# Channel means of the edge filter as f32 products in 32-column groups, and tables of two layers loaded one stage earlier

## The chip, the cores and the metric

The kernel runs on one core of a Trainium2 chip. The metric is the device time of one execution in microseconds (us), lower is better. Three timed executions of the kernel before are shown, and one more was taken with the profiler.

## The reference, cut to what matters

The input x is 16 images of 32 channels of 64x64 in f32. Four layers are applied in turn, each as `x = x + conv(groupnorm(x))` with 16 groups of two channels. The convolutions are a spectral mixing (L0), the edge filter (L1), a 5x5 filter (L2) and a full-size circular filter (L3). The change is in L1. From the normalised x (here `x`) it takes

```python
x_mean = x.mean(axis=1, keepdims=True)                 # over the 32 channels
gx = conv(x_mean, sobel_x); gy = conv(x_mean, sobel_y) # 3x3, zero padding
edge = jnp.sqrt(gx * gx + gy * gy + 1e-06)
edge_strength = edge.reshape(B, 1, ht, P, wt, P).mean(axis=(3, 5))   # P = 8
edge_strength = edge_strength - edge_strength.min(axis=(2, 3), keepdims=True)
edge_norm = edge_strength / (edge_strength.max(axis=(2, 3), keepdims=True) + 1e-06)
edge_coeff = 1.0 + EDGE_BOOST * edge_norm
...
xf = jnp.fft.rfft2(x_patch)          # 8x8 patches
xf = xf * mask * scaling             # scaling from edge_coeff, per patch
out = jnp.fft.irfft2(xf, s=(P, P))
```

So the edge map of an image needs the mean over its channels at every pixel before the first patch can be filtered.

## The kernel before, in words

All of x stays in the on-chip tile `X`, 128 partitions (4 images by 32 channels) by Q = 4 groups by 4096 pixels. Each layer's normalisation is two numbers per partition and group, `rstd` (scale) and `shift`, so that the normalised value is `X * rstd + shift`. The program is a row of stages. Each stage is a block with one hand-written queue for each engine, and no engine enters the next block before all have left this one. In order: kernel spectra (with the statistics of the input), statistics `n0`, L0 forward, L0 mix, L0 inverse (`i0`), statistics `n1`, edge stage, L1 filter stage, statistics `n2`, L2, statistics `n3`, L3 forward, L3 mix, L3 inverse. Since the order inside a stage is written out by hand, nothing moves unless the code moves it.

`stats_stage` makes `rstd` and `shift` by one small product on PE and seven small steps on DVE and ACT. On SP it can also load tables (`loads`) and copy tiles (`copies`), and SP then waits for all of them. `n1` gets seven tables of the edge filter and four copies of the L2 weights, `n3` gets six tables of L3.

The edge stage (`l1_edge_stage`) goes through 32 chunks of 512 pixels, group by group. For each chunk ACT normalises into `e1_src` (L278), DVE rounds it to f16 into `hi` (L1229, shown as `e_high_part`), and DVE (even chunks) or POOL (odd ones) takes the rest `lo16` (L1195, `e_low_part`). PE multiplies each part by a 128-column window of the table `wide` in f16 that puts the means of this group's four images and of this strip of eight rows on the right 4 of 128 partitions (L1165); two narrow products of 64 columns fetch the rows above and below for the strips next to it (L1169, L1172). All sums are in PSUM banks 0 and 1. Ahead of them stand 16 transposes that only keep PE busy (`keep_warm`, L210). When all four groups are done, DVE copies the sums into `m` (L1234, L1235), with a frame of zeros, and the Sobel filter, the root, minimum and maximum follow in a row of small dependent steps that ends with the copy into `edge` (L1269).

`l0_forward_stage` collects its results in two halves by turns (`xm[q % 2]`): one is a tile of its own, the other lies in `y`.

In names of the trace `e_`, `ks_`, `f_`, `l_`, `i_`, `m_`, `c_` are prefixes of tiles by stage, `bank` is PSUM.

## Time and profile before

| | us |
|---|---|
| three timed executions | 951.16, 938.11, 948.60 |
| their median | 948.6 |
| the profiled execution, whole | 947.15 |
| its span, first to last instruction | 945.3 |
| outside the span (947.15 - 945.3) | 1.85 |
| mean granted TensorE clock | 0.923 of full |

The profiled execution lies 1.45 us below the median. The three timed ones lie 13 us apart. The stages in question stand in the span at 316.5 to 324.6 us (`n1`), 324.6 to 378.3 us (edge stage) and 641.1 to 645.8 us (`n3`).

### The profile page before, as it was taken

How to read it: one execution, taken by the hardware profiler on the slowest of the kernel's cores; microseconds unless marked ns; L12 is line 12 of the kernel's file. 1: busy time of each engine (PE TensorE's matmuls, PEld its weight loads, DVE VectorE, ACT ScalarE, POOL GpSimd, SP SyncE). 2: the span in 40 equal slices, each digit the busy share in tenths (PEclk: the TensorE clock that was granted, in tenths of full speed). 3: DMA queues.
4: the chain of work that ended last, by engine and by line, in shares of the span. 5: the costliest groups of instructions: out<-in, count | busy, mean ns of one | idle time of the engine just before them, and what ended most of it. 6: DMA issues, size and time to landing. Idle time of an engine off the chain costs nothing. (4 is left out here: it accounts for less than half of the span.)

```text
span 945.3 us, 28083 instructions
## 1 busy us (share of the span) xinstructions
PE 775.2 (82%) x11423; PEld 647.9 (69%) x11423; DVE 620.4 (66%) x1144; ACT 480.7 (51%) x800; POOL 108.9 (12%) x96
## 2 busy tenths in 40 slices
PE   7999996874699464887599999966888489889997
PEld 7999995764588342766444444435777488889997
DVE  3455445778476697689687776775666677756453
ACT  0133336864434270754579997005887557764200
POOL 0000000110100162456003223000000100000000
PEclk9999998997699797899799999997999888999985
DMA  8599968750000100000000000004000448840054
GB/s 314 199 316 383 314 200 213 184 117 4 2 0 0 41 1 0 2 0 0 1 1 1 1 1 1 1 1 107 1 0 0 89 91 176 180 89 1 1 206 155
DMA packets 48380, 80.25 MB, mean 85 GB/s; under 512 B 19874, under 2 KB 38312, under 8 KB 43448
## 3 DMA queue, kind: packets, MB, share of 16 engines
q1 hardware_dynamic: 31672, 62.49, 23.8%
q10 hardware_dynamic: 16640, 16.78, 5.2%
q8 instruction: 52, 0.85, 0.4%
q14 instruction: 16, 0.13, 0.0%
HBM read 50.74 MB, written 27.92 MB: 83 GB/s over the span
## 5 line engine op out<-in xcount | busy, mean ns | idle before, releaser
L1618 DVE SCALAR_TENSOR_TENSOR X<-bank,c_power,X 32x512 f32 x128 | 96.7, 756 | 36.5 <-PE bank L1568 32.9
L1761 PE MATMUL bank<-m_xp,m_kf 128*32 128x64 f32 x2048 | 81.4, 245 | 22.2 <-DVE m_xp L1696 11.1
L1761 PEld LDWEIGHTS bank<-m_xp,m_kf 128*32 128x32 f32 x2048 | 80.3, 171 | 23.4 <-issue 23.3
L415 DVE COPY ks_rows<-bank 128x512 f32<-128x512 f32 x64 | 41.3, 687 | 67.3 <-PE bank L345 67.3
L215 DVE BATCH_NORM_STATS2 bn<-X 128x6 f32 x128 | 83.0, 683 | 2.9 <-POOL X L1358 1.6
L433 ACT COPY ks_spec<-bank 128x512 f32<-128x512 f32 x64 | 34.3, 589 | 98.8 <-PE bank L360 96.1
L1524 ACT ACTIVATE c_r<-X,c_nrm 32x1024 f32 (+1 forms) x56 | 75.0, 1340 | 2.4 <-DVE c_nrm L1592 1.1
L345 PE MATMUL bank<-ks_fw,ks_src 64*128 64x64 f32 x1024 | 68.7, 298 | 6.3 <-DMA ks_src<-in_L_conv_weights 6.3
L360 PE MATMUL bank<-ks_fh,ks_rows 64*128 64x128 f32 (+1 forms) x1152 | 72.5, 281 | 0.2 <-ACT ks_spec L433 0.2
L345 PEld LDWEIGHTS bank<-ks_fw,ks_src 64*128 64x128 f32 x1024 | 68.1, 215 | 6.2 <-issue 6.2
L360 PEld LDWEIGHTS bank<-ks_fh,ks_rows 64*128 64x128 f32 (+1 forms) x1152 | 67.6, 184 | 3.3 <-issue 1.8
L620 DVE TENSOR_TENSOR f_tl<-bank,f_th 128x512 f16<-128x512 f32 x64 | 42.3, 682 | 19.3 <-ACT f_th L571 19.3
L1782 ACT COPY xm<-bank 64x512 f32 (+1 forms) x64 | 33.0, 595 | 39.1 <-PE bank L1761 39.1
L1568 PE MATMUL bank<-c_rh,c_w_high_odd 128*64 128x512 f16 (+1 forms) x288 | 48.0, 385 | 3.8 <-DVE c_rl L1510 3.8
L1568 PE MATMUL bank<-c_rh,c_w_high 128*64 128x512 f16 (+1 forms) x288 | 48.4, 387 | 1.6 <-DVE c_rl L1510 1.6
L488 PE MATMUL bank<-c_l_fw,f_th 128*128 128x64 f16 (+1 forms) x256 | 37.5, 207 | 13.1 <-DVE f_tl L620 13.1
L1568 PE MATMUL bank<-c_rh,c_w_low 128*64 128x512 f16 (+1 forms) x288 | 47.7, 382 | 0.0
L1568 PE MATMUL bank<-c_rl,c_w_high 128*64 128x512 f16 (+1 forms) x288 | 47.6, 382 | 0.0
L1309 PE MATMUL bank<-mm,p_tt 64*128 64x128 f32 x512 | 38.7, 293 | 10.8 <-DVE X L1341 6.7
L1568 PE MATMUL bank<-c_rl,c_w_high_odd 128*64 128x512 f16 (+1 forms) x288 | 47.6, 382 | 0.0
L1568 PE MATMUL bank<-c_rh,c_w_low_odd 128*64 128x512 f16 (+1 forms) x288 | 47.5, 382 | 0.0
L630 DVE TENSOR_TENSOR f_cl<-bank,f_ch 128x512 f16<-128x512 f32 x48 | 32.3, 688 | 22.5 <-ACT f_ch L585 22.4
(201 smaller groups left out, 1838.9 us busy)
## 6 DMA issues: line engine op xcount, KB each, us to landing
ks_src<-in_L_conv_weights SPq DMA_DIRECT2D x16, 1024.0 KB, 6.9
kf<-ks_spec ACTq DMA_DIRECT2D x16, 1024.0 KB, 8.9
m_kf<-kf SPq DMA_DIRECT2D x32, 512.0 KB, 8.4
X<-in_x SPq DMA_DIRECT2D x4, 2048.0 KB, 12.6
out_y<-X SPq DMA_DIRECT2D x32, 256.0 KB, 2.5
l_wb<-in_L_conv_weights_r SPq DMA_DIRECT2D x4, 512.0 KB, 11.1
l_wb<-in_L_conv_weights_i SPq DMA_DIRECT2D x4, 512.0 KB, 13.7
xf<-f_xm SPq DMA_DIRECT2D x16, 112.0 KB, 3.2
```

The costliest lines, as they stand in the source:

```text
L215: dve.bn_stats(self.bn[:, c, :], self.X[:, q, c * CH:(c + 1) * CH]).then_inc(step, 1)
L345: last = pe.matmul(ps[2 * g + r][:, c * N:(c + 1) * N], src[p][at, C // 4 * g + c, m], fw[at], start=True, stop=True)
L360: return pe.matmul(banks[j][0:slots * C, to:to + P], rows[p][half, m, at:at + slots].rearrange("p s c -> p (s c)"), mats[half, part], star ...
L415: dve.tensor_copy(rows[p][:, m, :, C // 2 * g + r:C // 2 * (g + 1):2], ps[2 * g + r][:].rearrange("p (c n) -> p n c", n=N)).then_inc(rows_ ...
L433: c = act.copy(spec[p][:, 2 * u:2 * u + 2, :, j:IB:2].rearrange("p f t m k -> p f m t k"), ps[4 + 2 * (u % 2) + j][:].rearrange("p (f m t ...
L488: pe.matmul(to, h, m[:, 0], start=True, stop=False)
L620: dve.tensor_tensor(self.tl[j % 4][:], ps[j % 4][:], self.th[j % 4][:], ALU.subtract).then_inc(self.turned_read, 1)
L1309: m = pe.matmul(ps[2 + 2 * (j % 2) + h][:, k * P:(k + 1) * P], tt[j % 2][at, k * P:(k + 1) * P], mm[at, :, at], start=True, stop=True)
L1524: act.activation(to, of, ACT.Identity, scale=nrm[at, 0, bass.ds(q, 1)], bias=nrm[at, 1, bass.ds(q, 1)]).then_inc(ready[b], 1)
L1568: return pe.matmul(ps[2 * n + (oy + odd) % 2][2 * oy * C:2 * (oy + 1) * C, :], w[rows, ky, kx, 2 * oy:2 * oy + 2].rearrange("p o c -> p (o ...
L1618: dve.scalar_tensor_tensor(x, of.rearrange("p (y x) -> p y x", x=HN), filt.power[at, 2:3], x, ALU.mult, ALU.add).then_inc(added, 1)
L1761: last = pe.matmul(ps[4 * half + m // 8][at:at + C, m % 8 * N:(m % 8 + 1) * N], kf[p][:, j, :, H * half + m], xp[half][:, j, m].rearrange( ...
```

## The change

It has three parts.

1. The means are made from `X` itself, in f32. The weights are the table `wide` times `rstd` of the group (four DVE steps, before any product), so scale and mean are one product; the part of `shift` is one number per image, made by four one-column products with a new table `l1_shift`, and added by DVE when the sums leave PSUM (`sh`, with a new table `l1_rows` that leaves it out beyond the border). The weights are 32 columns wide instead of 128: strip s writes only the 32 partitions of its pair of strips, in the order s = 0, 2, 4, 6, 1, 3, 5, 7, so that one product after another goes to another group of 32 columns. ACT's normalising, DVE's rounding and the low parts on DVE and POOL are gone.
2. The tables and copies of `n1` are issued by SP at the start of the stage before (`inverse_stage`), and the six tables of `n3` at the end of SP's queue in the first stage.
3. To make room for L3's tables, `xm` of `l0_forward_stage` lies wholly in `y`, and ACT's wait for the stores of the kernel spectra stands ahead of q = 0 instead of q = 1.

```diff
@@ l0_forward_stage
-        xm = [pr.sb(ctx, "f0_xm", [P, 2, S, KX, 2, IB]),
-              y.rearrange("p t x r b -> p (t x r b)")[:, 0:size].rearrange(
-                  "p (t s x r b) -> p t s x r b", t=2, s=S, x=KX, r=2)]
+        xm = [y.rearrange("p t x r b -> p (t x r b)")[:, g * size:(g + 1) * size].rearrange(
+            "p (t s x r b) -> p t s x r b", t=2, s=S, x=KX, r=2) for g in range(2)]
...
-                    if s == 0 and q == 1:
+                    if s == 0 and q == 0:
@@ inverse_stage, SP
+                for t, n in loads:
+                    sp.dma_start(t[:], pr.ins[n]).then_inc(next_const, 16)
+                for to, of in copies:
+                    sp.dma_start(to, of).then_inc(next_const, 16)
+                sp.wait_ge(next_const, 16 * (len(loads) + len(copies)))
@@ l1_edge_stage, ACT
-                with act.Fori(0, Q) as q:
-                    for j in range(NCH):
-                        act.wait_ge(split[j % 2], START + HC * (q - 1) + j // 2 + 1)
-                        pr.normalise(act, src, q, j, ready)
@@ l1_edge_stage, PE
                 pr.keep_warm(pe, 16)
-                pe.wait_ge(zeroed, 3)
...
-                            w = wq[p][:, 124 - B * s:124 - B * s + P]
-
-                            pe.wait_ge(split[s % 2], START + HC * q + s // 2 + 1)
-                            for part in (hi, lo16):
...
+                order = [2 * g + k for k in range(2) for g in range(PS // 2)]
+
+                def mean(q, s, to, of):
+
+                    at = slice(s // 2 * 2 * B, (s // 2 + 1) * 2 * B)
+                    first = 124 - s % 2 * B
+                    return pe.matmul(to[at, :], wq[:, q, first:first + 2 * B], of, start=q == 0 and s in started,
+                                     stop=False, skip_group_check=True)
+
+                for q in range(Q):
+                    pe.wait_ge(window, q + 1)
+                    rows = pr.X[:, q, :].rearrange("p (h w) -> p h w", w=N)
+                    started = (0, 2, 4, 6)
+                    for s in order:
+                        mean(q, s, ps[0], pr.X[:, q, s * CH:(s + 1) * CH])
+                    started = (1, 2, 4, 6)
+                    for s in order:
+                        if s > 0:
+                            mean(q, s, ps[1][:, 0:N], rows[:, ROWS * s - 1, :])
+                    started = (0, 2, 4, 6)
+                    for s in order:
+                        if s < PS - 1:
+                            last = mean(q, s, ps[6][:, 0:N], rows[:, ROWS * s + ROWS, :])
+                for q in range(Q):
+                    last = pe.matmul(ps[3][:, 0:1], shift_m[:, q * P:(q + 1) * P], pr.shift[:, q:q + 1],
+                                     start=q == 0, stop=q == Q - 1)
+                last.then_inc(meant, 1)
@@ l1_edge_stage, DVE
+                for q in range(Q):
+                    dve.tensor_scalar(wq[:, q], wide[:, 12 - IB * q:12 - IB * q + 252], pr.rstd[:, q:q + 1], None,
+                                      ALU.mult).then_inc(window, 1)
...
-                        for j in range(NCH):
-                            at = slice(j * CH, (j + 1) * CH)
-                            dve.wait_ge(ready, NCH * q + j + 1)
-                            dve.tensor_copy(hi[:, q, at], src[:, at]).then_inc(high, 1)
-                            if j % 2:
-                                low_part(dve, q, j - 1)
-                dve.wait_ge(meant, START + Q)
+                dve.wait_ge(meant, 1)
+                dve.tensor_scalar(sh[:], shift_rows[:], ps[3][:, 0:1], None, ALU.mult).then_inc(zeroed, 1)
                 dve.wait_ge(zeroed, 3)
-                dve.tensor_copy(m[:, 1:1 + ROWS, 1:1 + N], ps[0][:].rearrange("p (h w) -> p h w", w=N))
...
+                dve.tensor_scalar(m[:, 1:1 + ROWS, 1:1 + N], ps[0][:].rearrange("p (h w) -> p h w", w=N),
+                                  sh[:, 0:1], None, ALU.add)
+                dve.tensor_scalar(m[:, 0, 1:1 + N], ps[1][:, 0:N], sh[:, 1:2], None, ALU.add)
+                then(dve.tensor_scalar(m[:, HALO - 1, 1:1 + N], ps[6][:, 0:N], sh[:, 2:3], None, ALU.add))
@@ four_layers
-                kernel_spectra_stage(pr, fwd_loads + inv_loads, filt)
+                kernel_spectra_stage(pr, fwd_loads + inv_loads + last_loads, filt)
...
-                pr.stats_stage("n1", mean_loads + table_loads, filt.odd_copies())
+                pr.stats_stage("n1")
...
-                pr.stats_stage("n3", fwd_loads + inv_loads)
+                pr.stats_stage("n3")
```

On DVE the edge stage begins like this in the kernel before (L1204 is the stage's start; the tiles `e_` are its own). Of the two groups written out in the loop the first rows stand here:

```order
L1214 MEMSET e_m 128x660
L1215 MEMSET e_eps 128x1
L1216 MEMSET e_nought 128x256
L1220 UNCONDITIONAL_BRANCH
L1220 ISA
L1225 REGISTER_ALU
L1225 ISA
L1225 COPY e_wq<-c_l_mean 128x252
L1228 ISA
L1229 ISA
L1229 COPY e_high_part<-e_src 128x512
```

and like this in the changed kernel, up to the first step of the Sobel filter:

```order
L1196 TENSOR_SCALAR e_wq<-c_l_mean,rstd 128x252 x4
L1198 MEMSET e_m 128x660
L1199 MEMSET e_eps 128x1
L1201 TENSOR_SCALAR e_sh<-c_l_rows,bank 128x3
L1203 TENSOR_SCALAR e_m<-bank,e_sh 128x8x64
L1205 TENSOR_SCALAR e_m<-bank,e_sh 128x64
L1206 TENSOR_SCALAR e_m<-bank,e_sh 128x64
L1208 SCALAR_TENSOR_TENSOR e_v<-e_m 128x640
```

The weights of all four groups come first now, no chunk step is left, and three additions of `sh` stand where two copies stood.

PE's queue in the edge stage of the kernel before, from the transposes to the second chunk's first part:

```order
L210 MATMUL bank<-ident 128x128 x16
L1152 MATMUL bank<-e_nought 128x512
L1153 MATMUL bank<-e_nought 128x128
L1155 UNCONDITIONAL_BRANCH
L1155 ISA
L1162 ISA
L1165 ISA
L1165 MATMUL bank<-e_high_part,e_wq 128x512
L1165 REGISTER_ALU
L1165 MATMUL bank<-e_low_part,e_wq 128x512
L1165 ISA
L1165 MATMUL bank<-e_high_part,e_wq 128x512
```

and in the changed kernel, from the transposes to the product with the gains:

```order
L215 MATMUL bank<-ident 128x128 x16
L1147 MATMUL bank<-X,e_wq 32x512 x8
L1147 MATMUL bank<-X,e_wq 32x64 x14
L1147 MATMUL bank<-X,e_wq 32x512 x8
L1147 MATMUL bank<-X,e_wq 32x64 x14
L1147 MATMUL bank<-X,e_wq 32x512 x8
L1147 MATMUL bank<-X,e_wq 32x64 x14
L1147 MATMUL bank<-X,e_wq 32x512 x8
L1147 MATMUL bank<-X,e_wq 32x64 x14
L1165 MATMUL bank<-shift,c_l_shift 128x1 x4
L1170 MATMUL bank<-e_gain,c_l_band 128x1
```

There are 32 wide products instead of 64 and 56 narrow ones instead of 112, with 32 output partitions each, in one run without a wait for another engine's chunk.

SP's queue in the changed kernel from the start of `i0` (L837) to the gains of the edge stage:

```order
L837 UNCONDITIONAL_BRANCH
L840 DMA c_l_mean<-in_l_mean 128x264
L840 DMA c_l_pick<-in_l_pick 128x128
L840 DMA c_l_spread<-in_l_spread 16x512
L840 DMA c_l_shift<-in_l_shift 128x512
L840 DMA c_l_rows<-in_l_rows 128x3
L840 DMA c_l_dft<-in_l_dft 128x128
L840 DMA c_l_same<-in_l_same 128x128
L840 DMA c_l_band<-in_l_band 6x128
L840 DMA c_l_high<-in_l_high 128x1
L842 DMA c_w_high_odd<-c_w_high 64x1152
L842 DMA c_w_low_odd<-c_w_low 64x1152
```

These stood between the branches of `n1` before, without `c_l_shift` and `c_l_rows`.

## Rows read from the trace of the kernel before

**Rows 1.** Busy time of the engines while the means are made

```profile
core 0: us, PE busy (x) PEld busy (x) DVE busy (x) ACT busy (x) POOL busy (x), PEclk, DMA share, GB/s
324.57:363.50 38.93, 26.46 (x195) 17.82 (x195) 36.68 (x55) 24.40 (x32) 22.76 (x16) 0.94 0.00 1
```

**Rows 2.** Groups of instructions by form between 324 and 364 us

```profile
L1229 DVE CAST e_high_part<-e_src 128x512 f32 x32 | 23.6, 775 | 0.0
L1195 DVE TENSOR_TENSOR e_low_part<-e_src,e_high_part 128x512 f32 x16 | 10.9, 678 | 0.0
L1225 DVE CAST e_wq<-c_l_mean 128x252 f16 x4 | 4.0, 990 | 0.2 <-issue 0.2
```

**Rows 3.** Timeline in order of time, n1 into the edge stage

```profile
318.56 0.16 DVE L270 SCALAR_TENSOR_TENSOR shift<-gm,rstd 128x4 f32<-128x4 f32 x1
...
321.53 0.60 SPq L243 DMA_DIRECT2D c_w_low_odd<-c_w_low  x1
...
324.61 3.65 PE L210 MATMUL bank<-ident 128*128 128x128 f32 x16 [7.43 <-PEq L237]
```

**Rows 4.** Timeline, n2 into L2, where n2 loads nothing

```profile
455.89 0.16 DVE L270 SCALAR_TENSOR_TENSOR shift<-gm,rstd 128x4 f32<-128x4 f32 x1
...
456.35 5.77 PE L210 MATMUL bank<-ident 128*128 128x128 f32 x26 [1.84 <-PEq L237]
```

**Rows 5.** Timeline, n3 into L3 forward

```profile
643.14 0.16 DVE L270 SCALAR_TENSOR_TENSOR shift<-gm,rstd 128x4 f32<-128x4 f32 x1
643.43 0.43 SPq L241 DMA_DIRECT2D c_l_iw<-in_l_iw  x1
...
645.83 1.91 DVE L609 TENSOR_SCALAR f_src<-X,rstd,shift 128x512 f32<-128x512 f32 x4 [2.53 <-PEq L237]
```

**Rows 6.** Timeline, the end of the means

```profile
363.37 0.19 PE L1172 MATMUL bank<-e_low_part,e_wq 128*128 x1
...
363.60 0.69 DVE L1234 COPY e_m<-bank 128x512 f32<-128x512 f32 x1 [1.91 <-PE bank L1172]
...
364.52 0.83 DVE L1238 SCALAR_TENSOR_TENSOR e_v<-e_m 128x640 f32<-128x640 f32 x1
```

**Rows 7.** PE's timeline, f32 products: weights of 128 columns, then two halves of the rows

```profile
304.04 7.07 PE L916 MATMUL bank<-c_l_iw,i_tt 128*128 128x256 f32 x32
...
384.34 1.16 PE L1309 MATMUL bank<-mm,p_tt 64*128 64x128 f32 x16
```

**Rows 8.** PE's timeline, L3 mix: f32 products with 32-column weights

```profile
805.78 9.70 PE L1761 MATMUL bank<-m_xp,m_kf 128*32 128x64 f32 x256 [1.79 <-DMA m_kf<-kf]
```

**Rows 9.** Busy time in stretches of L1761 (762 to 775) and L1054 (898, 918)

```profile
762.50:775.00 12.50, 12.50 (x334) 12.40 (x332) 10.55 (x24) 10.43 (x16) 0.00 (x0) 1.00 0.47 97
...
898.00:902.00 4.00, 4.00 (x153) 4.00 (x149) 0.70 (x2) 0.00 (x0) 0.00 (x0) 1.00 0.02 4
918.00:922.00 4.00, 4.00 (x82) 4.00 (x84) 2.48 (x4) 0.00 (x0) 0.00 (x0) 0.50 0.50 184
```

**Rows 10.** Busy time of L1568's instructions alone (f16, 512 columns, two 64-column groups)

```profile
500.00:510.00 10.00, 10.00 (x110) 4.90 (x108) 1.00 0.01 2
```

**Rows 11.** Busy time at the start of the edge stage, after it, in i0

```profile
325.00:328.90 3.90, 3.90 (x19) 3.40 (x18) 3.67 (x9) 3.90 (x6) 1.39 (x1) 0.51 0.01 2
328.92:363.00 34.08, 21.65 (x171) 13.65 (x170) 32.77 (x47) 20.39 (x27) 21.37 (x15) 1.00 0.00 1
...
250.00:316.00 66.00, 58.40 (x382) 53.39 (x380) 41.64 (x76) 26.26 (x48) 4.29 (x12) 0.97 0.00 0
```

**Rows 12.** Timelines of SP, PE and ACT, first stage to L0 forward

```profile
120.71 0.43 SPq L330 DMA_DIRECT2D c_l_iw<-in_l_iw  x1
...
145.84 0.36 PE L249 MATMUL bank<-st,pair 128*128 128x8 f32 x2 [2.75 <-PEq L307]
...
152.24 0.34 SPq L670 DMA_DIRECT2D l_wb<-in_L_conv_weights_r  x1
...
166.22 0.36 ACT L715 COPY f_xm<-bank 128x224 f32<-128x224 f32 x1
```

More of the change, by code:

```diff
@@ L132, in constants @@
     out["l1_mean"] = wide
+    image = np.arange(P) // C
+    out["l1_shift"] = np.concatenate([np.tile(np.eye(B)[IB * q + image] / C, (1, PS)) for q in range(Q)], 1)
+    strip = np.arange(P) // B
+    out["l1_rows"] = np.stack([np.ones(P), strip > 0, strip < PS - 1], 1)
     out["l1_pick"] = np.stack([np.eye(P)[:, 16 * s:16 * s + 16] for s in range(PS)], 1).reshape(P, P)
@@ L802, in _, with inverse_stage @@
                 pool.memset(y[:, :, KX:].rearrange("p s x r b -> p s (x r b)"), 0.0)
-def inverse_stage(pr, name, y, slots, modes, mats, rows4, last):
+def inverse_stage(pr, name, y, slots, modes, mats, rows4, loads, copies):
     nc, ps = pr.nc, pr.psum
@@ L823, in inverse_stage @@
                                               ("made", "made_read", "turned2", "turned2_read"))
-    pixels, added, step, stored = (pr.sem(f"{name}_{n}") for n in ("pixels", "added", "step", "stored"))
+    pixels, added, step, next_const = (pr.sem(f"{name}_{n}") for n in ("pixels", "added", "step", "next_const"))
     padded = pr.sem(f"{name}_padded")
-    out_groups = pr.out.rearrange("(q b) c h w -> q (b c) (h w)", b=IB)
     with ExitStack() as ctx:
@@ L835, in _ @@
             def _(sp):
-                if last:
-                    with sp.Fori(0, Q) as q:
-                        for part in range(4):
-                            sp.wait_ge(added, START + NCH * q + NCH // 4 * (part + 1))
-                            at = slice(part * PIX // 4, (part + 1) * PIX // 4)
-                            sp.dma_start(out_groups[q][:, at], pr.X[:, q, at]).then_inc(stored, 16)
-                    sp.wait_ge(stored, 16 * 4 * Q)
+                for t, n in loads:
[3 more added lines that the diff above has]
+                sp.wait_ge(next_const, 16 * (len(loads) + len(copies)))
             def stage(eng, q, s):
@@ L930, in _ @@
                         dve.tensor_tensor(x, x, ps[4 + c % 4][:], ALU.add).then_inc(added, 1)
-                        if not last and c:
+                        if c:
                             dve.wait_ge(added, START + NCH * q + c)
                             pr.chunk_stats(dve, q, c - 1, step)
-                    if not last:
-                        dve.wait_ge(added, START + NCH * q + NCH)
-                        pr.chunk_stats(dve, q, NCH - 1, step)
-                        pr.group_stats(dve, q, step)
+                    dve.wait_ge(added, START + NCH * q + NCH)
+                    pr.chunk_stats(dve, q, NCH - 1, step)
+                    pr.group_stats(dve, q, step)
             @block.scalar
@@ L1109, in l1_edge_stage @@
     nc, ps = pr.nc, pr.psum
-    ready, window, meant = (pr.sem(f"e1_{n}") for n in ("ready", "window", "meant"))
+    window, meant = (pr.sem(f"e1_{n}") for n in ("window", "meant"))
     seq, root, picked, spread = (pr.sem(f"e1_{n}") for n in ("seq", "root", "picked", "spread"))
-    zeroed, high = pr.sem("e1_zeroed"), pr.sem("e1_high")
-    split = [pr.sem(f"e1_split{p}") for p in range(2)]
-    HC = NCH // 2
+    zeroed = pr.sem("e1_zeroed")
     gained, mask, mats = (pr.sem(f"e1_{n}") for n in ("gained", "mask", "mats"))
@@ L1117, in l1_edge_stage @@
     with ExitStack() as ctx:
-        src = pr.sb(ctx, "e1_src", [P, PIX])
-        hi, lo16 = (pr.sb(ctx, f"e1_{n}", [P, Q, PIX], F16) for n in ("high_part", "low_part"))
-        wide, pick, spread_m = means
+        wide, pick, spread_m, shift_m, shift_rows = means
         dft, same, band, high_mask = tables
         gain, mk, md = pr.sb(ctx, "e1_gain", [NB, 1]), pr.sb(ctx, "e1_mk", [P, 2]), pr.sb(ctx, "e1_md", [P, 2, P])
-        wq = [pr.sb(ctx, f"e1_wq{p}", [P, 252], F16) for p in range(2)]
+        wq = pr.sb(ctx, "e1_wq", [P, Q, 252])
+        sh = pr.sb(ctx, "e1_sh", [P, 3])
         m = pr.sb(ctx, "e1_m", [P, HALO, N + 2])
@@ L1131, in l1_edge_stage @@
         sq_eps = pr.sb(ctx, "e1_eps", [P, 1])
-        nought = pr.sb(ctx, "e1_nought", [P, CH], F16)
         with nc.Block() as block:
@@ L1190, in _ @@
                 last.then_inc(spread, 1)
-            def low_part(eng, q, j):
-                at = slice(j * CH, (j + 1) * CH)
-                eng.wait_ge(high, NCH * q + j + 1)
-                eng.tensor_tensor(lo16[:, q, at], src[:, at], hi[:, q, at], ALU.subtract).then_inc(split[j % 2], 1)
-            @block.gpsimd
-            def _(pool):
-                pool.sem_inc(split[1], START)
-                with pool.Fori(0, Q) as q:
-                    for j in range(1, NCH, 2):
-                        low_part(pool, q, j)
             @block.vector
```

52 lines of the change are left out of this document (12 added, 40 removed).

## The prediction

> **What bounds the kernel now.** The stages follow one another, with a barrier between them, so I read the two places that change on their own. First the busy time of the engines while the means are made [rows 1]: of 38.93 us DVE works 36.68, PE 26.46, ACT 24.40, POOL 22.76. The groups by form say on what [rows 2]: 32 roundings for 23.6 us, 16 low parts for 10.9, four tables for 4.0, together 38.5, the whole stretch. So DVE ends the means, and PE is fed by it. Then the timelines of the statistics stages. In `n1` the last arithmetic step, `shift`, starts at 318.56, but SP is still issuing at 321.53 and PE comes into the edge stage at 324.61 [rows 3]. In `n2`, the same stage with nothing to load, the step at 455.89 is followed by PE at 456.35 [rows 4]. In `n3` it stands at 643.14 and DVE starts at 645.83 [rows 5]. These waits for tables are bare time of the whole chip.
>
> **Part 1, tables out of n1 and n3.** From `shift` to the next stage n2 takes 0.46 us and n1 6.05 [rows 3, 4]: 5.6 us go. n3 takes 2.69 [rows 5]: 2.2 us go. What they cost elsewhere: SP does nothing in `i0`, and the DMA engines are idle there for 66 us (share 0.00) [rows 11]; nine loads and four copies at about 0.5 us of issue each need 7 us. In the first stage six more tables stand behind SP's last issue at 120.71 us and need some 3 us, while the next stage starts at 145.84; SP's next work is at 152.24 [rows 12]. Both cost 0. If the first stage's DMAs were late by the whole 3 us, it would still be covered by the 20 us that are left.
>
> **Part 2, `xm` in `y`.** ACT now waits for the kernel spectra's stores before its first `xm` copy, which stands at 166.22; SP, which waits for the same stores, has gone on at 152.24 [rows 12]. 14 us of cover, cost 0.
>
> **Part 3, the means.** ACT's, DVE's and POOL's chunk work goes away, and PE's own products become the path. PE starts at 319.0 (324.61 less 5.6), the 16 transposes take 3.65 us [rows 3], and the four DVE steps for the weights are done by then (even at the 0.99 us of the old ones [rows 2]; probably less). So products start at 322.7. Each group has 8 wide products (512 columns) and 14 narrow ones (64), all f32.
>
> An f32 product shows as two records: L916 has 16 products and 32 records of 256 columns in 7.07 us, 0.221 us each [rows 7]. For 512 columns that is 0.442 a record, 0.884 a product, if nothing overlaps. How much do the 32-column groups overlap? The nearest rows:
> - L1761 has the same form (128 rows, 32 columns of weights, f32), two groups by turns, 64 columns: 256 records in 9.70 us, 0.038 each [rows 8]. Without overlap 64 columns would be 0.055. Overlap 1.46.
> - L1309, two halves of the rows by turns, 128 columns: 16 records in 1.16 us, 0.073 each with the tail, against 0.110 [rows 7]. At least 1.5, nearer 2 in the steady part.
> - L1054, four row groups by turns, 64 columns: 153 records in 4.00 us, 0.026 each [rows 9]. Overlap 2.1, although four groups are there.
> - L1568, f16, 512 columns, two 64-column groups: 110 records in 10.00 us [rows 10], 0.091 each. One f16 pass of 512 columns is half of an f32 record, 0.221: overlap 2.4 (some records have fewer rows or are missing), so two full streams over 128 rows do run side by side.
>
> I take 2: wide streams like L1568's hide what is fixed in each record, and nothing with f32 goes above 2.1, with four groups by turns either. An order that would give such a cap: the two records of one product go to the same group, one after the other, and if starts keep the program's order, only the second record of one product meets the first of the next. A wide product is then 0.442 us and a narrow one 0.076 (two of L1761's records). Per group 8 x 0.442 + 14 x 0.076 = 4.60 us, four groups 18.4 us.
>
> Here the Trainium skill has a rule, "TensorE: Matmul & The Clock Gate", Part 3 (packing small matmuls): products in different 32-column tiles run at once, three of them 2.38 times as fast, and matmuls start and end strictly in order. By the 2.38 a wide product would take 0.37 us and the four groups some 16 us, an estimate from that page; no row here shows more than 2.1 with f32. The order it states is the one just described. That all tiles run at once is the rival "four at once" below.
>
> To add: the clock. Before, the granted clock was 0.51 (the 1.2 GHz level) until 328.9, 4.3 us after PE's start, and 1.00 after that [rows 11]. With the same 4.3 us PE would be at half speed to 323.3, 0.6 us into the products; since the moment varies I add 1.0 us. The four one-column products and the way out of PE: 0.5 us, an estimate from the 0.36 us that the one narrow product of a statistics stage takes [rows 12]. Sum 18.4 + 1.0 + 0.5: PE is done at 342.6. Before, its last product starts at 363.37, and the first Sobel step follows at 364.52 [rows 6], 1.15 us later; of this 0.69 is the wide copy and the rest the small one and latencies. Afterwards there is one step more ahead (`sh`, some 0.2 us) and one narrow step more: 1.3 us. The Sobel step starts at 343.9 instead of 364.5, so 20.6 us go, the 5.6 of n1 among them. What is late next is the chain of small steps that ends in `edge`; it is unchanged.
>
> With n3: 20.6 + 2.2 = 22.8 us. From the span 945.3 that leaves 922.5, and with 1.85 outside it **924.3 us**. The profiled execution lies 1.45 below the median of the timed ones, so on that scale it would be 925.8; I keep 924.3, since three runs 13 us apart don't carry that difference. From no change a measurement of this kernel can tell about 2%, 19 us.
>
> **Rivals.**
> - *Four at once.* All four column groups stream together: 0.221 a wide product, narrow ones 0.038. 8 x 0.221 + 14 x 0.038 = 2.3 a group, 9.2 in all, 9.2 less: 915.1. For it: the order of the strips lets it happen. Against: L1054's 2.1 with four groups.
> - *Little overlap.* The overlap of the only row in the same form, 1.46, holds for wide ones too: 0.605 each, 5.9 a group, 23.6 in all, 5.2 more: 929.5. For it: same form; two f32 streams over all 128 rows are in no other row. With none at all it is 8 x 0.884 + 14 x 0.110 = 8.6 a group, 34.4, 16 more: 940.3, and only DVE's ceiling has been exchanged for PE's. Against: L1761 itself is above 1.
> - *Slower than before: half clock and no overlap.* L1054, with a quarter of the rows at work, fell from clock 1.00 to 0.50 in the middle of its run and from 153 to 82 records in 4 us [rows 9]. If the 32-column products do that to PE while also serialised, a group costs 17.2 us and the means 68.8, 49.4 more than in my sum with its 1.0 for the clock: 973.7. It decides from 63 us for the means on (19.9 in my sum, 43 more); up to there the time is within 2% of before. Against: L1761, also with 32 columns, ran 12.5 us at 1.00 [rows 9]. Half clock with overlap would be 36.8, 17.4 more: 941.7, no slower than before.
> - *The loads don't leave the path*, because a table is late in its new place: 7.8 us less gained, 932.1. The idle DMA engines of `i0` speak against it.
>
> **How the numbers follow.** Forecast (overlap near 2) 0.60; four at once 0.12; overlap about 1.46 0.13; none, or half clock with overlap 0.09; loads stay on the path 0.03; half clock and no overlap 0.03 (slower). Beside these the end of the kernel is not steady: L1054 loses its clock at some moment, and in the whole of that stage a record costs 0.026 or 0.049 us, so with 1024 records it can move the time by some 10 us either way, about what the three runs show. So the forecast's own range is 917 to 932; with four at once below and little overlap above, the range for 8 in 10 is 913 to 936. Faster by over 2% means under 929.6. The forecast gives that with 0.85, four at once always, overlap 1.46 half the time: 0.51 + 0.12 + 0.07, that is 0.70. Slower by over 2%: 0.03. The rest, 0.27, is within 2%.
>
> **What the profile of the changed kernel would show.** From `shift` to PE's transposes 0.5 us in n1 and n3, as in n2. ACT and POOL idle during the means, DVE with four short steps. 64 wide and 112 narrow records of f32 on PE, the wide ones 0.22 us apart (0.11: four at once; 0.30: little; 0.44: none), and from the first to the last product some 19 us. DVE's wait for PE ahead of `sh` is the longest of the stage. A first Sobel step 25 us after PE's first transpose, against 40 before. The granted clock back at 1.00 within 5 us of PE's start. What would make me wrong: records further apart than 0.3 us, a clock of 0.5 through the products, or SP still busy when `i0` ends.

## The result, and the profile after

| | before | after |
|---|---|---|
| timed executions | 938.1 to 951.2, median 948.2 (4) | 905.4 to 914.1, median 909.8 (4) |
| ratio of the times | | 0.9618, 95% interval 0.9547 to 0.9689 |
| profiled execution, its span | 947.15, 945.3 | 905.9, 904.1 |
| mean granted clock | 0.923 | 0.938 |

The changed kernel is 38 us faster in this set. I had forecast 924.3 with a range of 913 to 936. Ratios and their intervals, here and below, leave out executions that lie more than 1.5% above the fastest of their kernel; the medians and spreads in the tables take in all.

The timeline of the kernel after, from the end of `n1` to the first Sobel step (start, duration, engine, line, operation; in brackets the idle time before it and its releaser):

```profile
316.46 0.16 DVE L275 SCALAR_TENSOR_TENSOR shift<-gm,rstd 128x4 f32<-128x4 f32 x1
...
316.93 3.65 PE L215 MATMUL bank<-ident 128*128 128x128 f32 x16 [1.84 <-PEq L242]
316.93 1.13 DVE L1196 TENSOR_SCALAR e_wq<-c_l_mean,rstd 128x252 f32<-128x252 f32 x4 [0.31 <-PEq L242]
...
320.50 8.86 PE L1147 MATMUL bank<-X,e_wq 128*32 128x512 f32 x176
...
322.25 0.57 PEld L1147 LDWEIGHTS bank<-X,e_wq 128*32 128x32 f32 x32 [0.30 <-issue]
323.01 0.23 PEld L1147 LDWEIGHTS bank<-X,e_wq 128*32 128x32 f32 x4 [0.20 <-issue]
323.44 0.23 PEld L1147 LDWEIGHTS bank<-X,e_wq 128*32 128x32 f32 x4 [0.20 <-issue]
323.87 0.23 PEld L1147 LDWEIGHTS bank<-X,e_wq 128*32 128x32 f32 x4 [0.20 <-issue]
...
329.29 1.05 PE L1165 MATMUL bank<-shift,c_l_shift 128*128 128x1 f32 x8
...
330.38 0.23 DVE L1201 TENSOR_SCALAR e_sh<-c_l_rows,bank 128x3 f32<-128x3 f32 x1 [11.61 <-PE bank L1165]
330.64 0.75 DVE L1203 TENSOR_SCALAR e_m<-bank,e_sh 128x512 f32<-128x512 f32 x1
...
331.81 0.83 DVE L1208 SCALAR_TENSOR_TENSOR e_v<-e_m 128x640 f32<-128x640 f32 x1
```

Set beside the rows of before:

- From `shift` to PE's first transpose: 0.47 us, as in `n2` (0.46 [rows 4]); before it was 6.05 [rows 3]. 5.6 us are gone.
- All 176 records of the means take 8.86 us. The weight loads (`PEld`) show how: in the wide products four loads come in one go, and the next four 0.43 us later (the row of 32 loads holds the 28 narrow ones of a group of images and four wide ones). 0.43 us is what one wide record takes (L916's 0.221 for 256 columns [rows 7], doubled, is 0.44). So four records of 512 columns run side by side, one in each of the four groups of 32 columns of the array. Sixteen such fours are 6.9 us, and 2.0 are left for the 112 narrow ones.
- From PE's first transpose to the first Sobel step: 14.9 us, against 39.9 (364.52 less 324.61 [rows 3, 6]). 25.0 us are gone.

The clock, in windows of the kernel after (length, busy time of PE, PEld, DVE, ACT, POOL with instruction counts, granted clock, DMA share, GB/s): half speed ends 0.1 us before the products begin.

```profile
313.60:320.40 6.80, 4.04 (x18) 3.78 (x18) 3.10 (x14) 0.30 (x1) 0.00 (x0) 0.50 0.01 1
320.40:329.30 8.90, 8.90 (x178) 5.66 (x177) 0.00 (x0) 0.00 (x0) 0.00 (x0) 1.00 0.01 2
```

SP's queue, in the stages that the tables went to, and the start of L3:

```profile
122.48 1.25 SPq L335 DMA_DIRECT2D c_l_fw<-in_l_fw  x1
...
127.36 0.43 SPq L335 DMA_DIRECT2D c_l_iw<-in_l_iw  x1
150.99 0.34 SPq L674 DMA_DIRECT2D l_wb<-in_L_conv_weights_r  x1
...
244.64 0.36 SPq L840 DMA_DIRECT2D c_l_mean<-in_l_mean  x1
...
250.55 0.60 SPq L842 DMA_DIRECT2D c_w_low_odd<-c_w_low  x1
...
611.24 0.16 DVE L275 SCALAR_TENSOR_TENSOR shift<-gm,rstd 128x4 f32<-128x4 f32 x1
...
611.71 1.46 DVE L614 TENSOR_SCALAR f_src<-X,rstd,shift 128x512 f32<-128x512 f32 x3 [0.31 <-PEq L242]
```

L3's tables are issued from 122.48 to 127.8 (5.3 us, where I had some 3), 23 us before SP's next work; `n1`'s take 6.5 us at the start of `i0`, which lasts another 60. In `n3` 0.47 us lie between `shift` and DVE, 2.69 before [rows 5]: 2.2 us gone.

The three places give 5.6 + 25.0 + 2.2 = 32.8 us. The span is 41.2 shorter. The difference lies in the last stage, which the diff doesn't touch. Groups of PE by form there (busy time, mean ns | idle before), of before and then of after:

```profile
L1054 PE MATMUL bank<-c_l_iw,xm 32*128 32x64 f32 x1024 | 40.3, 331 | 2.0 <-issue 1.2 <-ACT xm L1070 0.8
```

```profile
L1053 PE MATMUL bank<-c_l_iw,xm 32*128 32x64 f32 x1024 | 30.9, 274 | 3.1 <-issue 2.4 <-ACT xm L1069 0.8
```

The same 1024 records cost 9.4 us less, and the stage, from its first product to the end, took 38.5 us instead of 47.9. Windows over the stage, before and then after:

```profile
897.40:916.00 18.60, 17.32 (x600) 17.08 (x603) 9.92 (x16) 0.00 (x0) 0.00 (x0) 1.00 0.56 205
916.00:945.30 29.30, 22.93 (x432) 22.74 (x428) 9.92 (x16) 0.00 (x0) 0.00 (x0) 0.50 0.44 161
```

```profile
865.60:897.30 31.70, 29.30 (x1006) 28.63 (x1009) 17.36 (x28) 0.00 (x0) 0.00 (x0) 1.00 0.62 225
897.30:904.10 6.80, 1.55 (x26) 1.36 (x22) 2.48 (x4) 0.00 (x0) 0.00 (x0) 0.50 0.56 206
```

Before, the clock fell after 18.6 us and some 430 records ran at half speed; after, it fell when 26 were left. 32.8 + 9.4 = 42.2; the rest together is 1.0 us slower: up to `shift` of `n1` 2.1 us faster, from the Sobel step to `shift` of `n3` 0.8 slower, and from L3's start to the last stage's first product 2.3 slower. Whether the 9.4 us belong to the change, or are chance, is one of the questions of the experiments.

### The profile page after: what moved, and what is told of

Same layout as the page of the kernel before. It is cut to its first block and busy times, and to the rows that moved or that the text cites. A ratio compares the mean times of both kernels' runs of the same rounds, so it can differ in the third digit from the quotient of the medians.

```text
span 904.1 us, 27651 instructions
## 1 busy us (share of the span) xinstructions
PE 755.6 (84%) x11429; PEld 633.2 (70%) x11429; DVE 586.3 (65%) x1097; ACT 456.1 (50%) x768; POOL 86.2 (10%) x80
## 5 line engine op out<-in xcount | busy, mean ns | idle before, releaser
L1588 DVE SCALAR_TENSOR_TENSOR X<-bank,c_power,X 32x512 f32 x128 | 96.8, 756 | 36.5 <-PE bank L1538 32.8
L420 DVE COPY ks_rows<-bank 128x512 f32<-128x512 f32 x64 | 41.2, 687 | 66.6 <-PE bank L350 66.6
L438 ACT COPY ks_spec<-bank 128x512 f32<-128x512 f32 x64 | 34.4, 589 | 97.4 <-PE bank L365 97.4
L625 DVE TENSOR_TENSOR f_tl<-bank,f_th 128x512 f16<-128x512 f32 x64 | 42.2, 683 | 18.9 <-ACT f_th L576 18.8
L1538 PE MATMUL bank<-c_rh,c_w_high 128*64 128x512 f16 (+1 forms) x288 | 48.4, 387 | 1.9 <-DVE c_rl L1480 1.9
L1328 POOL TENSOR_TENSOR X<-X,p_tmp 128x512 f32 x32 | 40.5, 1272 | 96.5 <-DVE X L1311 96.5
```

The source lines that it names most:

```text
L420: dve.tensor_copy(rows[p][:, m, :, C // 2 * g + r:C // 2 * (g + 1):2], ps[2 * g + r][:].rearrange("p (c n) -> p n c", n=N)).then_inc(rows_ ...
L625: dve.tensor_tensor(self.tl[j % 4][:], ps[j % 4][:], self.th[j % 4][:], ALU.subtract).then_inc(self.turned_read, 1)
L1328: pool.tensor_tensor(x, x, tmp[j % 2][:].rearrange("p a (y x) -> p a y x", x=PS), ALU.add).then_inc(finished, 1)
L1538: return pe.matmul(ps[2 * n + (oy + odd) % 2][2 * oy * C:2 * (oy + 1) * C, :], w[rows, ky, kx, 2 * oy:2 * oy + 2].rearrange("p o c -> p (o ...
L1588: dve.scalar_tensor_tensor(x, of.rearrange("p (y x) -> p y x", x=HN), filt.power[at, 2:3], x, ALU.mult, ALU.add).then_inc(added, 1)
```

## The experiments

Twelve runs were made, on four chips. Each row "before" is the kernel before on one chip, and the rows under it ran on that chip. "Products" is the row of the means' products on PE; "last stage" the time from its first product to the end, and in it the time at half clock, both of the profiled execution. Ratios are to the kernel before on the same chip.

| kernel | times, median (lowest to highest) | ratio, interval | products | last stage, at half clock |
|---|---|---|---|---|
| before | 943.3 (939.0 to 950.6) | | | |
| after again | 913.5 (910.0 to 929.4) | 0.965, 0.955 to 0.975 | 8.9 | 44.5, 23.7 |
| tables_only | 933.7 (925.2 to 946.2) | 0.986, 0.976 to 0.996 | | 49.6, 35.0 |
| means_only | 933.7 (924.9 to 939.6) | | 8.85 | 48.9, 34.4 |
| strips_in_line | 924.0 (917.8 to 930.7) | 0.977, 0.967 to 0.988 | 8.88 | 58.8, 55 |
| before | 943.1 (936.8 to 950.5) | | | |
| full_width | 943.1 (one) | | 40.08 | 42.4, 18.0 |
| half_width | 916.8 (one) | | 17.22 | 40.6, 12.7 |
| side_products | 943.6 (one) | | 8.85 | 58.7, 54.8 |
| shift_first | 915.6 (907.5 to 928.2) | 0.967, 0.959 to 0.975 | 10.93 | 37.1, 2.3 |
| before | 944.7 (934.8 to 952.9) | | | |
| end_transposes | 910.7 (908.4 to 911.9) | 0.968, 0.961 to 0.974 | 8.86 | 39.8, 2.3 |
| after, third set | 927.0 (915.9 to 928.5) | 0.981, 0.972 to 0.991 | 8.9 | 58.8, 55 |
| before | 944.6 (934.8 to 956.2) | | | |
| before_end | 944.2 (940.4 to 947.0) | 1.004, 1.000 to 1.007 | | 40.4, 5.1 |
| end_two | 909.7 (908.8 to 934.8) | 0.964, 0.952 to 0.976 | 8.9 | 38.2, 4.2 |

### What each part is worth

The kernel after, unchanged:

> The changed kernel once more, as the control of this row of runs. Its profiled execution was 41.2 us shorter in the span than the one before, of which 33 us lie at the three places of the change and 8.3 us in the last stage, where the clock fell at another moment. Theory (the last 8 us are chance): timed executions fall in two heaps near 905.5 and 914, and the median difference to before is 33 to 40 us. Rival (the change itself shortens the last stage): each profile of the changed kernel has a last stage some 8 us shorter than before.

The times ran from 910.0 to 929.4, not in two heaps near 905.5 and 914, and the medians differ by 29.7 us, less than the 33 to 40 expected. The last stage took 44.5 us here, 38.5 in the first profile of the same kernel and 58.8 in the third (below), against 47.9 before. So the 9.4 us are chance and not a gift of the change.

Then the tables alone. It is the kernel after with the edge stage of before, and without `l1_shift` and `l1_rows` in the loads:

```diff
@@ four_layers, of the kernel after
-                                                         ("l1_spread", [B, Q * P]), ("l1_shift", [P, Q * P]),
-                                                         ("l1_rows", [P, 3])])
+                                                         ("l1_spread", [B, Q * P])])
```

> Only parts 1 and 2 of the change: the tables and copies leave n1 and n3, xm lies in y, the edge stage is the old one. Theory (each part acts at its own place and the gains add): n1 is 5.6 us and n3 2.2 us shorter, 7.8 us less than before in all, near 940. Rival (loading tables early also helps or hurts elsewhere): a difference beyond 7.8 by more than the 4 us that one comparison leaves open, or i0 or the first stage longer.

And the means alone: the kernel before with the new edge stage, whose two tables are loaded in `n1` with the others.

```diff
@@ four_layers, of the kernel before
-                                                         ("l1_spread", [B, Q * P])])
+                                                         ("l1_spread", [B, Q * P]), ("l1_shift", [P, Q * P]),
+                                                         ("l1_rows", [P, 3])])
```

> Only part 3: the edge stage of the changed kernel, with its two new tables loaded in n1, which keeps its loads. Theory: from PE's start to the first Sobel step 14.9 us instead of 39.9, 25 us less, minus about 0.9 us for the two more loads in n1: near 924. The clock at the products may be lower at their start, since the stage starts at another moment: up to 2 us. Rival: products are slower than in the changed kernel, for the clock, and the gain is under 22 us.

Timelines of `tables_only`, where the tables no longer stand in `n1`, and then of `means_only`:

```profile
318.71 0.16 DVE L275 SCALAR_TENSOR_TENSOR shift<-gm,rstd 128x4 f32<-128x4 f32 x1
...
319.17 3.47 PE L215 MATMUL bank<-ident 128*128 128x128 f32 x16 [1.84 <-PEq L242]
```

```profile
318.94 0.16 DVE L276 SCALAR_TENSOR_TENSOR shift<-gm,rstd 128x4 f32<-128x4 f32 x1
...
322.86 0.60 SPq L249 DMA_DIRECT2D c_w_low_odd<-c_w_low  x1
...
325.94 3.24 PE L216 MATMUL bank<-ident 128*128 128x128 f32 x15 [8.38 <-PEq L243]
```

Each part does its work by itself: the tables take `n1`'s wait to 0.46 us and leave the edge stage at 39.9; the means take 39.9 to 14.6 and leave the wait, now 7.0 with two more tables. So the waits add up: 7.8 us for the tables, 25 for the means. The whole times don't show it: both medians are 933.7, some 9.6 below before, where I had expected near 940 and near 924. The sets of `means_only` and `tables_only` spread over 15 and 21 us, and in `means_only`'s profiled execution stretches that no edit touches took more than in that of before: the last stage 48.9 for 47.9 us, L3's mix 94.2 for 92.2 from its first product to its last, and from there to the last stage's first product 50.0 for 48.4. I can't say more of the 9.6 than that. (`tables_only`'s own profile is of its longest execution, 944.4 us of span, so only the waits and the edge stage are read from it.)

### How many groups run at once

> The changed kernel with the strips in their natural order, 0, 1, 2 to 7, so that two products in a row go to the same group of 32 columns. Same products, same sums. Theory A (records start in the program's order, and a record waits for its own group): two products with four records follow each other in one group, and only at the change of a group two records overlap: 13 steps of 0.43 us per group of images for the wide ones, 5.6 instead of 1.7, and the products take about 25 us instead of 8.9: 16 us slower than the changed kernel. Theory B (PE takes any record whose group is free, as far as it looks ahead): no more than 2 us slower.

```diff
-                order = [2 * g + k for k in range(2) for g in range(PS // 2)]
+                order = list(range(PS))
```

```profile
322.13 8.88 PE L1147 MATMUL bank<-X,e_wq 128*32 128x512 f32 x176
...
322.59 0.15 PEld L1147 LDWEIGHTS bank<-X,e_wq 128*32 128x32 f32 x4 [0.28 <-issue]
323.02 0.15 PEld L1147 LDWEIGHTS bank<-X,e_wq 128*32 128x32 f32 x4 [0.28 <-issue]
```

In this order the four records of strips 0 and 1 all belong to the first group of columns. Had starts kept the program's order, three of four would have waited for the one before them, and the products would have taken some 25 us, as expected under theory A. They took 8.88 us, as in turn (8.86), and the loads come four in one go here too, 0.43 us apart. The theory of the prediction falls: a record that waits for its group does not hold up the records behind it, at least not three of them. The order "in turn" is worth nothing here.

The Trainium skill, "TensorE: Matmul & The Clock Gate", Part 3, says that matmuls start and end strictly in order. These two times (8.86 and 8.88 us) speak against it for starts of f32 records in different 32-column groups, and here the measurement decides; which of the two records of a product PE's queue holds where is not in the trace.

> The changed kernel with weights of 64 columns, two groups of columns by turns. Theory (as many wide records at once as there are groups): two at once, 64 x 0.43 / 2 plus narrow ones of about 0.027, the products take 16 to 18 us instead of 8.9. Rival (a cap of its own at two streams or at bandwidth decides, and four were only seen because of the small weights): the distance between half and full width is not a factor of two.

```diff
-                    at = slice(s // 2 * 2 * B, (s // 2 + 1) * 2 * B)
-                    first = 124 - s % 2 * B
-                    return pe.matmul(to[at, :], wq[:, q, first:first + 2 * B], of, ...
+                    at = slice(s // 4 * 4 * B, (s // 4 + 1) * 4 * B)
+                    first = 124 - s % 4 * B
+                    return pe.matmul(to[at, :], wq[:, q, first:first + 4 * B], of, ...
```

The order of the strips also changes, so that one product after another goes to the other half (`order = [4 * g + k for k in range(4) for g in range(2)]`).

> The changed kernel with weights of 128 columns (the whole window), so each product takes the whole array; the same f32 products otherwise. Theory (the gain over my sum is the four column groups at once): no two wide records overlap, 64 records of 0.43 to 0.44 us and 112 narrow ones of about 0.055, the products take 33 to 35 us instead of 8.9, and the first Sobel step comes 24 to 26 us later than in the changed kernel. Rival (f32 products on X are quick for another reason, the missing waits): under 15 us.

```diff
+                    first = 124 - B * s
+                    return pe.matmul(to, wq[:, q, first:first + P], of, ...
```

PE's timelines, of `half_width` with its weight loads, then of `full_width`:

```profile
321.89 17.22 PE L1147 MATMUL bank<-X,e_wq 128*64 128x512 f32 x176
...
322.81 0.14 PEld L1147 LDWEIGHTS bank<-X,e_wq 128*64 128x64 f32 x2 [0.28 <-issue]
323.23 0.14 PEld L1147 LDWEIGHTS bank<-X,e_wq 128*64 128x64 f32 x2 [0.28 <-issue]
```

```profile
322.55 40.08 PE L1146 MATMUL bank<-X,e_wq 128*128 128x512 f32 x176
...
323.41 0.19 PEld L1146 LDWEIGHTS bank<-X,e_wq 128*128 128x128 f32 x1 [0.24 <-issue]
323.84 0.19 PEld L1146 LDWEIGHTS bank<-X,e_wq 128*128 128x128 f32 x1 [0.24 <-issue]
```

Loads come every 0.43 us in all three, one at full width, two at half, four at a quarter: 17.22 is 1.94 times 8.86. Full width takes 2.3 times 17.22, not 2, and more than the 33 to 35 us that I had expected. Its 64 wide records at 0.43 are 27.5 us and leave 12.5 for 112 narrow ones, 0.11 each, twice their 0.055 of columns: I read this as a weight load of 128 columns that takes its own time and is not hidden behind so short a product. `full_width` also prices the other half of the change. With f32 products on `X` but the old width, the one execution took 943.1 us, as the kernel before. The tables' 7.8 us are gained in it; the edge stage, from PE's first transpose to the first Sobel step, takes 45.7 us, 5.8 more than before. So by itself the move from DVE to f32 products on PE is a loss, and the narrow weights make it a gain.

### Why L1054 and L1761 had shown less

Both had made me take an overlap of 2. Behind the means, four sets of 64 extra products with 64 columns of data were put, which write PSUM tiles that nothing reads:

```diff
+                for n in range(64):
+                    g = n % 2 * 32
+                    pe.matmul(ps[2][g:g + 32, 0:64], pr.X[:, 0, 0:32], pr.X[:, 1, 0:64], ...
+                for n in range(64):
...
+                    pe.matmul(ps[4][g:g + 32, 0:64], pr.X[:, 0, 0:2048:64], pr.X[:, 1, 0:64], ...
+                for n in range(64):
+                    g = slice(n % 4 * 32, n % 4 * 32 + 32)
+                    pe.matmul(four[n % 4][0:32, 0:64], pr.X[g, 0, 0:32], pr.X[g, 1, 0:64], ...
+                for n in range(64):
...
+                    pe.matmul(four[n % 4][:, 0:64], pr.X[g, 0, 0:128], pr.X[g, 1, 0:64], ...
```

> The changed kernel with 256 more f32 products of 64 columns behind the means, on results that nobody reads: 64 on 128 rows and 32 columns in two column groups by turns with weights side by side, 64 the same with weights 64 elements apart (as L1761 reads them), 64 on 32 rows and 32 columns in four row groups, 64 on 32 rows and 128 columns in four row groups (as L1054). 128 records each. Theory (the weight load of 128 columns held L1054 at 0.026 to 0.028 us a record, and the distance between weights held L1761 at 0.038): 0.027 for the first kind, 0.038 for the second, 0.014 for the third, 0.028 for the fourth. Rival (row groups never overlap more than twofold; 128 rows in two groups cost more in themselves): third kind 0.026 or more; first kind as slow as the second, 0.038.

```profile
333.80 3.77 PE L1171 MATMUL bank<-X 128*32 128x64 f32 x128
337.39 5.03 PE L1174 MATMUL bank<-X 128*32 128x64 f32 x128
342.36 1.97 PE L1177 MATMUL bank<-X 32*32 32x64 f32 x122
...
345.05 0.31 PE L1177 MATMUL bank<-X 32*32 32x64 f32 x6 [0.73 <-issue]
...
345.29 4.98 PE L1180 MATMUL bank<-X 32*128 32x64 f32 x128
```

- Two column groups with weights that lie together: 0.028 us a record (3.59 from start to start, by 128), a full 2. So it is the number of groups at work that counts: a 32-column record is not short in itself. The same with weights 64 elements apart, as a table that is cut across has them: 0.039. That is L1761's 0.038 [rows 8], whose weights lie 64 apart too. Their distance accounts for its 1.46.
- Four row groups (32 of the array's 128 rows each) with weights of 32 columns: 0.016, 3.4 at once, by the 122 records ahead of a pause of 0.7 us whose cause the trace doesn't show. With weights of 128 columns: at full clock 0.027 (below), L1054's 0.026 [rows 9]. So its 2.1 belongs to the 128 columns and not to a cap on row groups. PEld is busy all the time there (2.40 of 2.40 us), which points at the weight load; that the products also write 128 partitions instead of 32 was not told apart from it.

Windows of the last set, its first and its second half:

```profile
345.30:347.70 2.40, 2.40 (x90) 2.40 (x88) 0.00 (x0) 0.00 (x0) 0.00 (x0) 0.99 0.04 7
347.70:350.00 2.30, 2.30 (x52) 2.30 (x49) 0.00 (x0) 0.00 (x0) 0.00 (x0) 0.50 0.00 0
```

The granted clock fell to half within it, after the third set and half of the fourth, both on 32 rows.

### The head of the edge stage

The four one-column products and `sh` go ahead of the means, behind 4 transposes instead of 16:

```diff
-                pr.keep_warm(pe, 16)
+                pr.keep_warm(pe, 4)
+                for q in range(Q):
+                    moved = pe.matmul(ps[3][:, 0:1], shift_m[:, q * P:(q + 1) * P], pr.shift[:, q:q + 1],
+                                      start=q == 0, stop=q == Q - 1)
+                moved.then_inc(offset, 1)
...
```

> The changed kernel with the four one-column products ahead of the means instead of behind them, DVE's sh step with them, and 4 transposes instead of 16 ahead. Theory (they stand on the path, 1.05 us behind the products, 0.3 for sh; the 12 transposes are 2.7 us ahead): the first Sobel step comes 1.5 to 3 us earlier after the stage's start, less what products at half clock cost. In the whole time 2 us are hardly visible. Rival (without the 16 transposes the products run at half clock for 4 us and more): no gain or up to 2 us loss in the stage.

```profile
320.02 1.08 PE L215 MATMUL bank<-ident 128*128 128x128 f32 x4 [1.84 <-PEq L242]
320.89 1.71 PE L1142 MATMUL bank<-shift,c_l_shift 128*128 128x1 f32 x8
322.53 10.93 PE L1151 MATMUL bank<-X,e_wq 128*32 128x512 f32 x176
```

The products start 1.1 us sooner after the first transpose (2.5 instead of 3.6) and take 2.1 us longer, since the clock is at half until 326.8. From the first transpose to the Sobel step it is 14.7 instead of 14.9: of the 1.5 to 3 us expected nothing to speak of is won. The 16 transposes pay for themselves.

### The last stage

In the profiled executions of the same last stage it took 37.1 us with 2.3 of them at half clock, 38.5 with 6.8, 40.6 with 12.7, 47.9 with 29.3, and 58.8 with 55. That is near 36 us and 0.4 for each us at half clock. The profiled executions of `strips_in_line` and of the third set of the kernel after (926.6 and 926.7 us of span) are some 22.5 us longer than the first of the kernel after, and 20.3 of these lie in the last stage; so I put their medians of 924 and 927 down to it, not to the order of the strips. The last stage's products (32 rows of the array) were then given company:

```diff
                for c in range(NCH):
                    if c >= 2:
                        pe.wait_ge(added, Q * (c - 1))
+                    for _ in range(4):
+                        pe.transpose(ps[4 * (c % 2)][:, 0:P], pr.ident[:], pr.ident[:])
```

> This is the kernel after, with four more f32 transposes of the whole 128 x 128 identity written in front of the work of each of the last stage's 8 chunks (32 in all, about 0.1 to 0.2 us each, so 4 to 7 us of TensorE time; they go into a PSUM tile that the same step then overwrites). The question is whether the last stage, whose time from its first product to the end was 37.1 to 58.8 us in ten profiled executions of the same code, with 2.3 to 55 us of it at half clock, is held at full clock by more products of full size. Theory A (the clock stays up): under 5 us of the stage at half clock, the stage takes 37 to 43 us, and the times are about 905 to 910 us in every run. Rival B (the added products don't hold it): the clock falls somewhere in the stage as before, the stage takes the usual 37 to 59 us with the added time on top, and the median is 3 to 10 us above the kernel after's 910 to 914 us. The edge stage should be unchanged in both: products 8.9 us, from PE's start to the first Sobel step 14.9 us.

> The kernel after once more, unchanged, on the same chip as the run with added transposes, so that the two can be set beside each other. Expected: 906 to 914 us, ratio to the kernel before 0.955 to 0.970, the edge stage's products 8.9 us for 176 shown records, from PE's start to the first Sobel step 14.9 us, and the last stage anywhere from 37 to 59 us by how long it runs at half clock.

Groups of PE by form in the last stage, of the kernel after in its third set, and of `end_transposes`:

```profile
L1053 PE MATMUL bank<-c_l_iw,xm 32*128 32x64 f32 x1024 | 52.9, 402 | 1.4 <-ACT xm L1069 0.8 <-issue 0.6
```

```profile
L1055 PE MATMUL bank<-c_l_iw,xm 32*128 32x64 f32 x1024 | 30.8, 272 | 0.1
L1050 PE MATMUL bank<-ident 128*128 128x128 f32 x32 | 5.2, 286 | 0.8 <-ACT xm L1071 0.8
```

`end_transposes`, the window from its first product to its last:

```profile
869.20:904.60 35.40, 34.45 (x1053) 32.53 (x1052) 18.16 (x30) 0.00 (x0) 0.00 (x0) 1.00 0.58 211
```

The clock stayed at full speed until the last product was done, and all four times lay within 3.5 us, with mean granted clocks of 0.924 to 0.928. On the same chip the kernel after ran from 915.9 to 928.5, at 0.896 to 0.912. My expectation for that set (906 to 914) was wrong: I had trusted a median whose spread I knew. The two remaining runs asked whether this holds ahead of any code, and whether half of it does.

> This is the kernel before with the same four transposes ahead of each of the last stage's 8 chunks (32 in all, 5.1 us of TensorE time in the run of the kernel after with them, whose last stage took 39.8 us and whose four times lay within 3.5 us, 908.4 to 911.9). Theory A (the last stage's clock is what spreads this kernel's times, and the added transposes hold it up, whatever stands ahead in the program): last stage 38 to 41 us with under 6 us at half clock, times within some 5 us of each other, at 938 to 942 us, the lower end of the kernel before's 935 to 953; the distance to the kernel after with the same transposes is then a cleaner measure of the change, 29 to 33 us. Rival B (the narrow spread was luck, or the spread comes from other stages): times over 10 us apart again, and the last stage above 43 us.

> This is the kernel after with two transposes instead of four ahead of each chunk of the last stage (16 in all, half of the 5.1 us). Theory A (half the added work holds the clock too): last stage 37 to 39 us, under 6 us at half clock, median 906 to 909 us, 1 to 3 below the 910.7 of the run with four, times within 5 us. Rival B (two are too few): the clock falls in the stage in some or all runs, times spread over more than 10 us again, median 912 to 927 as in the sets of the kernel after (909.8, 913.5, 927.0).

```profile
L1056 PE MATMUL bank<-c_l_iw,xm 32*128 32x64 f32 x1024 | 30.4, 272 | 0.0
L1051 PE MATMUL bank<-ident 128*128 128x128 f32 x32 | 5.2, 286 | 0.8 <-ACT xm L1072 0.8
```

`before_end`, whose rows these are, has 30.4 us and 5.2, close to the 30.8 and 5.2 of `end_transposes`; its ten times lie within 6.6 us, those of the kernel before on that chip, 13 of them, within 21.4. Its median is no lower; I take it that part of the executions of before pay less for the clock than the transposes cost, but those executions have no profile. It was expected at 938 to 942 and came at 944.2: the best case of before is not what it returns to. Two transposes a chunk are too few: three times at 909 and one at 934.8. With the last stage tied down on both sides, the change is worth 944.2 - 910.7 = 33.5 us in the medians, and 943.67 - 910.83 = 32.8 in the profiled executions. The two ran on different chips; the kernel before had medians of 944.65 and 944.62 on them. The three places had given 32.8. The agreement is partly luck: in the execution of `before_end` the wait in `n3` alone was 1.1 us longer than in that of before (3.9 for 2.8, to PE).

## Why the prediction was wrong, step by step

- *Tables out of n1 and n3, 5.6 and 2.2 us:* right, each to 0.1 us, and by itself in `tables_only`. *Cost elsewhere 0:* no wait for a table is seen, but it is told to some 2 us only. From PE's first transpose after `n3` to the last stage, `before`, `means_only` and `before_end` took 251.5, 255.0 and 253.1 us, and the eleven traces with the tables moved 253.8 to 256.8. A cost of 1 or 2 us is not excluded.
- *`xm` in `y`, 0:* no wait for it is seen; from PE's start in L0 to `shift` of `n1` it was 170.5 to 171.3 us in the three traces without it and 169.6 to 173.0 in the eleven with it, which is as closely as this can be told.
- *PE starts, 3.65 us of transposes, weights done by then:* right; the four DVE steps took 1.13 us.
- *"I take 2":* **the step that failed.** The overlap is 4, and 18.4 + 1.0 us for the means became 8.9, the 9.2 of the rival "four at once" less a little. Both rows that I took for a cap had other causes, the 128-column weights in L1054 and the weights' distance in L1761, as the side products showed. Neither limited the wide products with 32-column weights. The order that I thought up to explain the cap was wrong as well, as `strips_in_line` showed: 8.88 us where it had asked for far more. I had the row that warned of it, L1568, whose two groups both streamed in full [rows 10]; the 2.4 that I read there is more than two groups can give, so I should have taken it for a full 2 out of 2.
- *The clock, 1.0 us:* 0 here, since it was back before the first product; `shift_first`, which started its products sooner, paid 2.1 us for it. What it costs is a matter of when the products start.
- *One-column products and PE's way out, 0.5 us:* 1.05 us. *The exit, 1.3:* 1.43, from the start of the `sh` step.
- *Forecast 22.8 us in all:* 32.8 at the places, and 33.5 with the last stage tied down. The forecast was thus about 10 us short by its own terms: 924.3 would have been 914.3 with 4 in place of 2, inside the range of 913 to 936. The other 8 us down to 905.9 are the last stage, which fell 9.4 us the right way in the execution shown. I had named that swing, 10 us either way, and the size was about right: 37.1 to 58.8 us is 11 either way of the 47.9 of before. But I joined it to the forecast alone; around the rival at 915.1 the range should have gone to 905.
- *Luck:* how far the whole time lay from 924.3 is in part chance. The two repeats of the kernel after had medians 29.7 and 17.7 us below before on their chips; taken from 948.2 that would be 918.5 and 930.5, inside the range, with the same step wrong.
- *The chances:* 0.12 for four at once against 0.60 was the wrong weight. A cap inferred from another shape is weak when the mechanism offered for it was not in any row.

## What to carry to other kernels

A row that shows less overlap than the groups allow says what limits that row: look at its weights, how many columns and how far apart, before it is taken for a limit of the engine. Where f32 products write few output partitions each, narrow weights in four 32-column groups can cut their time to a quarter and less of full width (8.86 us against 40.08), and their order didn't matter here. Where a stage of products on 32 rows loses its clock at another moment in each execution, some full-size transposes in it can narrow the spread (32 did, 16 failed once in four), and a change of 3% is then told with fewer runs.

## What the runs showed of the hardware that had not been expected

- 88 f32 products, 32 of 512 and 56 of 64 columns, took 8.86 us in 32-column groups, 17.22 in 64-column groups and 40.08 at full width.
- Records for a free column group pass at least three that wait for a busy one: 8.88 us in either order.
- With 64 columns of data and two 32-column groups, a record took 0.039 us where the elements of its weights lay 64 apart and 0.028 where they lay together; with 128-column weights and all 128 rows it took 0.11.
- The same last stage took 37.1 to 58.8 us; with 5.2 us of transposes in it, 39.8 and 40.4. What exactly tips the clock is open: `end_two` held it in its profiled execution (38.2 us), and one of its four times was 25 us longer.
